# The expert's first bias on TensorE: two 16-row products in the place of one product of zeros, and a gelu without a bias operand

## The reference

```python
t = t + attn(layernorm(t))   # a recurrence over the 256 positions, window of 5
t = t + ffn(layernorm(t))    # eight experts, the best two per token count

# the recurrence, one step (all 8 images at once)
temp   = tanh(H_prev @ W1 + (ht @ W2)[:, None, :] + H_prev_tilde @ W3)
w_t    = softmax(temp @ v, axis=1)
ht_til = ht + relu(sum(H_prev_tilde * w_t, axis=1))

# the experts
h = gelu(einsum('nd,edh->enh', xf, W1) + b1[:, None, :])   # exact gelu, hidden 256
o = einsum('enh,ehd->end', h, W2) + b2[:, None, :]
y = einsum('ne,end->nd', comb, o)                          # comb: top-2 probabilities
```

## Time and profile before

| | us |
|---|---|
| median of 3 runs | 613.19 |
| the three runs | 606.77, 614.01, 613.19 |
| the profiled execution's own time | 605.58 |
| its span in the profile | 603.6 |
| busy: PE, PEld | 543.0, 396.6 |
| busy: DVE, ACT, POOL | 474.9, 373.4, 59.6 |

### The profile page before, as it was taken

How to read it: one execution, slowest core, us unless ns; L and a number is a source line. 1 busy time by engine, 2 the same in 40 slices (tenths; PEclk the granted TensorE clock), 3 DMA queues, 4 the chain that set the end, 5 groups by cost and what they waited for, 6 DMA issues and landing times. The chain is left out here.

```text
span 603.6 us, 20624 instructions
## 1 busy us (share of the span) xinstructions
PE 543.0 (90%) x6808; PEld 396.6 (66%) x6808; DVE 474.9 (79%) x3364; ACT 373.4 (62%) x1425; POOL 59.6 (10%) x104
## 2 busy tenths in 40 slices
PE   6987639999999999999999999999999999999987
PEld 3643226666777776777767777677777767777766
DVE  2576577788888888888888888888888888888873
ACT  2356434456666676666666666666666666676664
POOL 1010170000000000001010101010101010100010
PEclk9686559999889999899999999999899999899999
DMA  8000000000000000000000000000000000000000
GB/s 229 7 2 0 0 2 1 3 2 3 3 6 3 7 3 8 2 8 2 8 3 6 3 7 2 8 2 7 3 6 3 7 3 8 1 8 3 7 1 10
DMA packets 7512, 5.90 MB, mean 10 GB/s; under 512 B 1216, under 2 KB 6896, under 8 KB 7408
## 3 DMA queue, kind: packets, MB, share of 16 engines
q1 hardware_dynamic: 6784, 4.57, 2.7%
q10 hardware_dynamic: 528, 0.03, 0.1%
q0 software_dynamic: 96, 0.00, 0.0%
HBM read 3.55 MB, written 1.05 MB: 8 GB/s over the span
## 5 line engine op out<-in xcount | busy, mean ns | idle before, releaser
L473 ACT ACTIVATE th<-bank 128x32 f32<-128x32 f32 x255 | 51.3, 201 | 133.5 <-PE bank L619 133.5
L944 DVE SCALAR_TENSOR_TENSOR DE<-CC,yh 128x40 f32<-128x40 f32 x509 | 100.9, 198 | 28.0 <-DVE yh L1008 1.8
L619 PE MATMUL bank<-Tp,vp 128*128 128x32 f16 x765 | 100.8, 183 | 19.3 <-DVE Tp L968 6.7
L727 PE MATMUL bank<-f,hid 128*128 128x128 f32 x512 | 116.0, 309 | 0.9 <-ACT hid L488 0.6
L492 ACT ACTIVATE GF<-Z,cst 64x32 f32<-64x32 f32 x255 | 103.7, 407 | 18.5 <-DVE Z L989 11.3
L940 DVE TENSOR_TENSOR_SCAN CC<-th,DE 128x16 f32<-128x16 f32 x510 | 112.8, 221 | 0.0
L693 PEld LDWEIGHTS bank<-GF,cst 128*128 128x128 f32 x510 | 77.5, 191 | 40.2 <-issue 38.9
L488 ACT ACTIVATE hid<-bank,b1T 128x128 f32<-128x128 f32 x256 | 94.0, 368 | 14.3 <-PE bank L619 6.6
L619 PE MATMUL bank<-xnT,f1p 128*128 128x128 f16 x1024 | 100.1, 221 | 0.2 <-ACT hid L488 0.2
L619 PEld LDWEIGHTS bank<-Tp,vp 128*128 128x128 f16 x765 | 69.7, 115 | 46.0 <-DVE Tp L968 24.2
L693 PE MATMUL bank<-GF,cst 128*128 128x32 f32 x510 | 96.7, 272 | 2.4 <-ACT GF L492 1.9
(11 more groups left out here) (140 smaller groups left out, 900.0 us busy)
## 6 DMA issues: line engine op xcount, KB each, us to landing
x_tok<-in_x_dram SPq DMA_DIRECT2D x4, 256.0 KB, 5.3
f<-in_L_ffn_W_dram SPq DMA_DIRECT2D x1, 1024.0 KB
out_dram<-acc SPq DMA_DIRECT2D x16, 64.0 KB
w<-in_L_attn_W_dram SPq DMA_DIRECT2D x3, 64.0 KB, 3.9
cst<-shape_constants_dram SPq DMA_DIRECT2D x1, 148.5 KB, 2.4
wfg<-in_L_conv_Wf_dram ACTq DMA_DIRECT2D x1, 8.0 KB, 2.6
wfg<-in_L_conv_Wg_dram ACTq DMA_DIRECT2D x1, 8.0 KB, 2.8
bhc<-in_L_conv_bh_dram POOLq DMA_DIRECT2D x1, 0.1 KB, 3.1
```

Of the source, the lines that this page charges most:

```text
L473: act.activation(th[p][:, 0:W4, 1], psS[p][:, 0:W4], ACT.Tanh, bias=-K0 / 2, scale=0.5 / WS).then_inc(th_ready, 1)
L619: mm = pe.matmul(out, weight[i], data[j], start=(start and n == 0), stop=(stop and n == len(which) - 1))
L727: mm = pe.matmul(psO[e % 2][:, 0:D], hid[u % 2][:, :], f2[:, u, :], start=(half == 0), stop=(half == HH - 1))
L944: return dve.scalar_tensor_tensor(DE[to][:, :, side].rearrange("p (w b) -> p w b", b=B), CC[frm][:, B:W5 + B, 1].rearrange("p (w b) -> p w ...
```

## The change

TensorE adds the bias inside the unit's PSUM accumulation. `b1_rows`, which holds unit u's 128 biases in row u, becomes a float16 pair `b1p` of 16 rows by 128 columns, scaled by 64; `row_of_unit` is a 16x16 identity in float16. A product of `b1p` with column u of `row_of_unit`, repeated over 128 columns, puts unit u's bias under every token; two products, one for each part of the pair, open the accumulation, and the four products of the unit add to it. In the recurrence the two stand where the one product of zeros stood, ahead of the wait for `GF`, behind a new wait for `gelu_done` (the previous unit's gelu has read the bank). Steps without a unit keep their products of zeros. In the tail the two stand directly ahead of the unit's four. The gelu's per-partition bias operand `b1T` goes away, and with it the transpose and the copy that made it; VectorE gets two splitting instructions on 16x128 and a copy of 16x16.

```diff
-        b1T = sb("b1T", [P, UNITS])
+        b1p = [sb(f"b1p_{i}", [UNITS, P], F16) for i in range(2)]
+        row_of_unit = sb("row_of_unit", [UNITS, UNITS], F16)
-        SPLITS = 4 * 2 + 2 + 2
+        SPLITS = 4 * 2 + 2 + 2 + 3
-                        act.activation(hid[u % 2][:, :], hidden(k, u), ACT.Gelu, bias=b1T[:, u:u + 1], scale=1 / WS
+                        act.activation(hid[u % 2][:, :], hidden(k, u), ACT.Gelu, scale=1 / WS
                                        ).then_inc(gelu_done, 1)
-                pe.transpose(bank[5][:, 0:E], wr_rows[:, :], ident[0:E, 0:E])
-                pe.transpose(bank[5][:, 64:64 + UNITS], b1_rows[:, :], ident[0:UNITS, 0:UNITS]).then_inc(wt_ps, 1)
+                pe.transpose(bank[5][:, 0:E], wr_rows[:, :], ident[0:E, 0:E]).then_inc(wt_ps, 1)
+            def unit_bias(out, u):
+                row = row_of_unit[:, u:u + 1].to_broadcast([UNITS, P])
+                pe.matmul(out, b1p[0][:, :], row, start=True, stop=False)
+                pe.matmul(out, b1p[1][:, :], row, start=False, stop=False)
...
-                        spin(psS[p], 1)
+                        if unit:
+                            if not (k == 1 and unit[2] == 0):
+                                pe.wait_ge(gelu_done, unit[1] + unit[2])
+                            unit_bias(hidden(k, unit[2]), unit[2])
+                        else:
+                            spin(psS[p], 1)
                         pe.wait_ge(g_ready, n)
                         pe.wait_ge(f_ready, n)
...
                     if unit:
                         jp, jb, u = unit
-                        if not before:
-                            if k == 1 and u == 0:
-                                pe.wait_ge(fsplit, 3)
-                            else:
+                        if not chain:
+                            if not before:
                                 pe.wait_ge(gelu_done, jb + u)
+                            unit_bias(hidden(k, u), u)
+                        if k == 1 and u == 0:
+                            pe.wait_ge(fsplit, 3)
                         product(hidden(k, u), [f1p[m][:, u * P:(u + 1) * P] for m in range(2)],
-                                [xnT[m][jp][:, :] for m in range(2)], True, True, ALL_PRODUCTS).then_inc(up_ps, 1)
+                                [xnT[m][jp][:, :] for m in range(2)], False, True, ALL_PRODUCTS).then_inc(up_ps, 1)
...
                     dve.wait_ge(wt_ps, 1)
-                    dve.tensor_copy(wrT[:, :], bank[5][:, 0:E]).then_inc(prep, 1)
-                    dve.tensor_copy(b1T[:, :], bank[5][:, 64:64 + UNITS]).then_inc(wt_sb, 1)
-                    dve.wait_ge(prep, 4)
-                    split2(wrT[:, :], wrp, done)
+                    dve.tensor_copy(wrT[:, :], bank[5][:, 0:E]).then_inc(wt_sb, 1)
+                    dve.wait_ge(wt_sb, 1)
+                    done = split2(wrT[:, :], wrp, done)
+                    dve.wait_ge(ld_ffn, 16 * 6)
+                    split2(b1_rows[:, :], b1p, done)
+                    dve.tensor_copy(row_of_unit[:, :], ident[0:UNITS, 0:UNITS]).then_inc(split, 1)
```

## The result

The changed kernel takes 732.51 us (median of 4 runs, 731.02 to 740.02) against 610.15 for the kernel before (4 runs): a ratio of 1.206, 95% interval 1.199 to 1.213. Its profiled execution is 731.02 us with a span of 728.9, 125.3 more than before.

A forecast was written before the change was run, and what follows sets the result against it. It took the 1.87 us step loop through VectorE's scans and `Z` to `GF` as the bound, gelu hidden. 605.6 - 1.4 + 0 + 0.2 + 0.1 + 19 = 623.5 us, raised for run spread to 627; range 604 to 650.

The forecast's parts named there:

- the term of the clock: Recurrence: 16-row products replace 128-row zeros, so TensorE's clock falls more often: +19 us, bounds 0 and +93.
- One in five of 233 is 47 steps: Recurrence: 47 of 233 steps hit by the low clock, a share taken from late tile-turn steps and five falls.
- The price: Recurrence: a step at clock 0.50 takes 2.34 us against 1.87; +0.4 us on the mean.
- rival 4: Recurrence: clock hardly comes back after the first fall, half to all steps low, 650 to 695 us; chance 0.05.
- The rows: Start, 20.0 to 26.6 us: TensorE busy throughout, clock stayed at 0.50, so 16-row products count little for it.
- The gelu: Without operand 0.10 us shorter, hidden in ordinary steps, whole in step 1 of tiles 2 to 15: -1.4 us.
- The two products in the slot: Recurrence: two 128-column products for one of 256 cost 0; bounds 0 and +0.12 a step, 0 and +28 us.
- rival 2: Recurrence: 16-row products or the new wait delay `GF`'s product by up to 0.12 us, 632 us; chance 0.06.
- The tail's small term: Tail: shorter gelu against two bias products, +0.02 a round, +0.2 us over some 11 rounds; bounds -1.1 and +4.6.
- The start's term: Start: VectorE gets three small instructions, loses a copy, mostly taken by a wait: +0.1 us, bounds 0 and +0.5.

The follow-up runs named there:

- no zeros: Kernel before, bias still in the gelu, without the product of zeros in steps with a unit and nothing in its place: 651.02 us.
- 16-row zeros: Kernel before, bias still in the gelu, product of zeros in steps with a unit on 16 rows instead of 128, same 256 columns: 722.84 us.
- The version with the zeros put back: Changed kernel with the 128-row product of zeros put back behind the two 16-row bias products in steps with a unit: 610.88 us, ratio 1.002.
- the 128-row version: Changed kernel with bias pair and selecting row padded with zeros to 128 rows: 604.08 us, ratio 0.989; timed again 606.95 us, ratio 0.993.
- the bursts of four at a tile's head: Changed kernel with four more products of zeros at the end of each of steps 0 and 1 of tiles 2 to 15: 758.43 us.
- the version with the gelu alone: Kernel before with only the gelu's bias operand taken away, product of zeros kept: 608.15 us, ratio 0.995.
- 128 rows with more zeros: Changed kernel with biases padded to 128 rows, plus a 128-column product of zeros ending steps 13, 15, 0, 1 and 2: 603.67 us, ratio 0.996.

## Why the prediction was wrong

It said 627 us, 604 to 650, slower with 0.50; it was 732.51. The direction and the place were right, the size was off by a factor of six in the term of the clock: +19 us for the steps, where the recurrence grew by 112.3.

- **The step that failed** is the count: "One in five of 233 is 47 steps". It was all of them from the second fall on, step 9 of tile 1: 231 steps. I took the share of low steps from the five falls of the kernel before, and with it, unsaid, that a fall ends after 3.4 us. The change did two things to that. The runs show each: without the 128-row zeros the clock falls every few tens of us (no zeros: 651 us); and with 16-row products in the queue it doesn't come back (16-row zeros: 723 us; the changed kernel). That the longer step at 0.50 is what keeps the clock from coming back is argued from these: with the ordinary low step at 2.13 to 2.16 it came back some 20 times in each of four kernels, with 2.34 not once in the recurrence by the ordinary work of five, and with 2.37 three times in one. Length alone doesn't decide: with the pair and the whole product of zeros together the one ordinary step wholly at 0.50 is 2.38 us long, low steps 0 and 3 up to 2.59, and the clock came back after 3.4 us in each of the four falls behind the first unit. It looks like the 128-row work set against the length; no run separated the two, and why the clock doesn't come back stays open so far.
- **The price** of a low step, +0.4, was too low as well. The step of 2.34 in the earlier trace rows was a step 0, with a transpose in it; an ordinary low step of the kernel before is 2.13, +0.26. In the changed kernel the same two are 2.55 and 2.34, since the 16-row columns add 0.21 to each. The mean is 112.3 / 231 = +0.49, with 3.17 us for step 13 against 2.09.
- **The tail** at 0.50 was not priced: +16.6 us. With it and the measured step, rival 4 (the clock hardly comes back, 0.05) would have reached 605.6 + 231 x 0.49 + 16.6 = 735. It named what happened, and its top of 695 was short by these two.
- **The rows** argument held in its conclusion and was weaker than I took it. From 20.0 to 26.6 the clock stayed low in the kernel before; in the changed kernel nearly the same start has it back at 23.5. What carries the conclusion is the pair of runs with zeros in 16 and in 128 rows.
- **The gelu** came out at 277 ns against 368, as said, and hidden by `Z` in ordinary steps. Step 1 gives 0.17 instead of 0.10: 14 x 0.17 = 2.4 us instead of 1.4. In the changed kernel itself nothing of it is left, since at 0.50 TensorE is the bound.
- **The two products in the slot** cost 0 at full clock, as said, and rival 2 is out: the step of 1.86 us above. At 0.50 they cost 0.21 where the zeros cost nothing, which I hadn't asked.
- **The tail's small term**, +0.02 a round, was mis-sized too. The version with the zeros put back shows the changed kernel's tail at full clock: 1.64 - 1.23 = +0.41 a round and 24.7 - 21.4 = +3.3 us in all, where +0.2 was taken and +4.6 was the bound. Few rows are why: in the 128-row version the tail is 597.9 - 575.9 = 22.0, +0.6 with a short fall of the clock in it.
- **The start's term** (+0.1) can't be read: starts of the same code differ by far more, as the last section shows.

## What to carry to other kernels

A product that computes nothing may be the one that holds TensorE's clock; before useful work takes its place, compare rows, not only columns and time. Judge the low state by its own queue: at 1.2 GHz another engine bounds the step, work that was hidden isn't, and whether the clock comes back there made a loss of 6% (no zeros, 651 us) into one of 20%. Narrow operands can be padded with zero rows: here that cost nothing in the recurrence, took the tail from 24.7 us to 22.0, and turned 1.206 into 0.993.

## What the runs showed of the hardware that was not expected

- **64 rows were no better than 16.** Products of 16, 64 and 128 rows with the same columns gave 732, 738 and 604 us (recurrences of 607.1, 603.9 and 491.2). At 0.50 the 64-row products take as much time as 16-row ones. Whether their rows count for a part all the same stays open: the falls at 148.7 and at 129.3 don't tell it. Open too is why the bursts of four at a tile's head never woke the clock, when TensorE's ordinary steps with the product of zeros always did in the kernel before.
- **Few-row products lie bare.** A following 128-row weight load starts beside a 128-row product (523.17 above) and behind a 16-row one (402.14); with 64 rows `GF`'s product comes as late as with 16 (0.50 us). At full clock a round of the tail is 0.41 us longer than before with 16-row products, 0.03 with 128-row ones.
- **Busy is not enough.** TensorE was busy 560.60 of 560.60 us at 0.50. The Trainium skill, TensorE: Matmul & The Clock Gate, "What's actually happening", puts the gate down to how busy the PE has been; this case's trace disagrees, unless rows are part of what is meant. The profile's length of a product tells nothing of rows: the 16-row product of 128 columns lasts 0.22 us at full clock (127.08 above), the 128-row one 0.22 (217 ns, the group's mean in the 128-row version).
- **A per-partition operand can cost twice**: 0.09 us of length, and behind the copy of step 1 the overlap with the instruction ahead (0.13 us). The Trainium skill, ScalarE: Activation LUTs, "What ACT_TABLE_LOAD costs", has both figures, some 93 ns for the operand and some 93 ns of overlap of neighbours; the trace agrees with the first, and has the second (0.11) for the gelu without operand behind the copy only.
- **The start varies more than the change is worth.** The first score's tanh starts at 87.47 us in the kernel before and at 95.25 in the version with the gelu alone, whose start is the same code; in the latter the clock is at 0.50 from 15.1 to 100.4 without a break. The recurrence by itself, first to last tanh, is the sharper measure: 494.8, 492.1, 491.2 and 490.4 us for before, gelu alone, 128 rows, and 128 rows with more zeros. The second profile of the 128-row version, 489.7, says how sharp: to 1.5 us, so that the last two don't differ.
